# Last expert subtractions ahead of the last norm, token numbers transposed a unit sooner, rank products in f16

## The reference

```python
x = x + wkv(w, u, layernorm(x), ctx)          # k = layernorm(x), v = ctx, recurrence over the 128 times:
#   no = max(o, u+k_t); y = (exp(o-no)*p + exp(u+k_t-no)*v_t) / (exp(o-no)*q + exp(u+k_t-no)); p, q, o updated
h = layernorm(x)                               # 2048 tokens of 512
probs = softmax(h @ gate_w.T)                  # 8 experts
weights, selected = top_k(probs, 2)
moe = sum over the 2 chosen experts e of weight_e * ((silu(h @ G_e.T) * (h @ U_e.T)) @ D_e.T)   # width 256
shared = sigmoid(h @ s.T) * ((silu(h @ G.T) * (h @ U.T)) @ D.T)                                 # width 1024
out = x + moe + shared
```

## Time and profile before

| | us |
|---|---|
| median of 3 timed runs | 570.06 (569.88 to 572.94) |
| the profiled execution | 573.75 |
| its span, first to last instruction | 570.1 |
| TensorE busy | 493.4 (87%) |
| VectorE busy | 423.6 (74%) |
| GpSimd busy | 342.1 (60%) |
| ScalarE busy | 276.4 (48%) |

### The profile page before, as it was taken

The page is one execution under the profiler, slowest core; times in us unless marked ns, Lnnn a source line. Parts: engine busy times, 40 slices in busy tenths (PEclk is TensorE's granted clock), DMA queues, the critical chain, the costliest instruction groups (busy, mean ns, idle before and its releaser), DMA issues.

```text
span 570.1 us, 10205 instructions
## 1 busy us (share of the span) xinstructions
PE 493.4 (87%) x2703; PEld 264.5 (46%) x2703; DVE 423.6 (74%) x954; ACT 276.4 (48%) x534; POOL 342.1 (60%) x421
## 2 busy tenths in 40 slices
PE   1116699899999999999999979899999999999970
PEld 1113345445555555455555544355545555555530
DVE  5778987999989899899898876466656665566650
ACT  4849837475674764756746433433323333333310
POOL 5767946757848578579485364315465665565432
PEclk9999989999999999999999999899999999999995
DMA  7960104115213223052101410305566866576352
GB/s 288 413 259 19 38 18 185 57 27 178 76 56 131 76 103 138 21 185 75 38 20 39 131 60 14 112 20 113 99 108 123 157 114 115 109 127 120 72 75 37
DMA packets 25929, 59.14 MB, mean 104 GB/s; under 512 B 6314, under 2 KB 6314, under 8 KB 24338
## 3 DMA queue, kind: packets, MB, share of 16 engines
q0 software_dynamic: 9824, 20.90, 20.7%
q1 hardware_dynamic: 16050, 37.59, 18.3%
HBM read 37.83 MB, written 20.65 MB: 103 GB/s over the span
## 4 chain that ended last, share of the span: by engine, by line
PE 54%; DVE 14%; issue 11%; POOL 6%; DMA 6%; ACT 5%; SPq 1%; POOLq 0%; DVEq 0%; ACTq 0%
PE GU L882 30%; PE DN L897 14%; DMA out<-wall,idsa 5%; PE XT L827 3%; PE HT L827 3%; ACT wall L700 3%; DVE st L1080 2%; DVE wall L1077 2%; DVE wall L1070 2%; DVE hb L1194 1%; POOL nrm L409 1%; DVE th L1191 1%; DVE xb L1095 1%; SPq L365 1%; POOL xb L572 1%
## 5 line engine op out<-in xcount | busy, mean ns | idle before, releaser
L882 PE MATMUL GU<-wall,xt 128*128 128x512 f16 x768 | 187.9, 385 | 2.1 <-DVE wall L1172 2.0
L897 PE MATMUL DN<-wall,hx 128*128 128x512 f16 (+1 forms) x618 | 151.8, 382 | 6.4 <-DVE hx L1199 4.5
L882 PEld LDWEIGHTS GU<-wall,xt 128*128 128x128 f16 x768 | 75.7, 101 | 70.3 <-issue 4.0
L582 POOL DMA_INDIRECT out<-wall,idsa x39 | 61.8, 1584 | 73.2 <-SPq L369 35.2
L657 ACT ACTIVATE hx<-HT 128x256 f16<-128x256 f32 x103 | 39.0, 379 | 134.3 <-PE HT L827 132.6
L897 PEld LDWEIGHTS DN<-wall,hx 128*128 128x128 f16 x618 | 60.4, 99 | 82.7 <-issue 8.1
L1199 DVE TENSOR_TENSOR hx<-HT,hx 128x256 f16<-128x256 f32 x103 | 43.1, 418 | 65.9 <-ACT hx L657 55.5
L652 ACT ACTIVATE th<-GU,scl 128x256 f32<-128x256 f32 x103 | 48.4, 470 | 77.9 <-PE GU L882 74.9
L882 PE MATMUL GU<-wall,kb 128*128 x240 | 61.4, 379 | 0.2 <-DVE kb L1373 0.2
L572 POOL DMA_INDIRECT xb<-xn_rows,idsi x39 | 40.2, 1030 | 33.1 <-DMA out<-xb 15.6
L882 PE MATMUL GU<-wall,xnb 128*128 x228 | 58.5, 379 | 0.6 <-DVE xnb L1373 0.6
(11 more groups left out here) (162 smaller groups left out, 755.3 us busy)
## 6 DMA issues: line engine op xcount, KB each, us to landing
wall<-wgu SPq DMA_DIRECT2D x12, 1024.0 KB, 9.8
wall<-wd SPq DMA_DIRECT2D x12, 512.0 KB, 10.4
out<-xb SPq DMA_DIRECT2D x20, 256.0 KB, 2.3
xb<-x SPq DMA_DIRECT2D x16, 256.0 KB, 2.8
cb<-ctx_t SPq DMA_DIRECT2D x16, 256.0 KB
xn_rows<-xnb SPq DMA_DIRECT2D x16, 256.0 KB
xb<-xn_rows,idsi POOLq DMA_INDIRECT x39
out<-wall,idsa POOLq DMA_INDIRECT x39
```

Of the source, the lines that this page charges most:

```text
L582: pool.indirect_dma_start(out, bass.IndirectOffsetOnAxis(ap=idsa[:, j:j + 1], axis=0), ye[j % RESULTS], None, compute_op=ALU.add).then_inc ...
L882: ins = nc.tensor.matmul(GU[par][:], lhs(xp, c), gate_up(base, wp, c), start=m == 0, stop=m == 3 * HC - 1)
L897: ins = nc.tensor.matmul(DN[:], hx[par][:, hp * IE + c * P:hp * IE + (c + 1) * P], down(base, wp, c), start=start and m == 0, stop=stop an ...
```

## The change

Four edits. The rank products (`ranks`) take f16 operands, tri16, all16 and an f16 mask, in place of f32 tri, ones and mask; all16 needs one more memset on GpSimd, and tri16 is cut from it. Pieces 1 and 2 of expert 6 (`expert_lo(E - 2, ..)`) stand on GpSimd ahead of the last second norm and of the scatter of tile 12. TensorE's transpose of the token numbers moves from after unit 61 into it, between its hidden transposes and its last six products. On VectorE the copy to yb moves up to stand right behind `experts_of_slots`, and idsi and idsa up to right behind hidden_lo 60; hidden 61 and the accumulate of tile 14 now come behind them.

```diff
-        ident, ones, tri = sb("ident", [P, P]), sb("ones", [P, P]), sb("tri", [P, P])
+        ident, ones = sb("ident", [P, P]), sb("ones", [P, P])
+        all16, tri16 = sb("all16", [P, P], F16), sb("tri16", [P, P], F16)
...
-        ones2, mask, pos2 = sb("ones2", [P, TOPK, E]), sb("mask", [P, E]), sb("pos2", [P, TOPK, E])
+        ones2, mask, pos2 = sb("ones2", [P, TOPK, E]), sb("mask", [P, E], F16), sb("pos2", [P, TOPK, E])
...
             def other_consts():
-                link(pool.affine_select(out=tri[:], in_=ones[:], compare_op=ALU.is_gt, fill=0.0,
+                link(pool.memset(all16[:], 1.0))
+                link(pool.affine_select(out=tri16[:], in_=all16[:], compare_op=ALU.is_gt, fill=0.0,
                                         base=0, pattern=[[1, P]], channel_multiplier=-1))
...
             turns(turn, LAG)
+            expert_lo(E - 2, 1)
+            expert_lo(E - 2, 2)
             norm(B - 1, 1, agg2, norm2, xn_rdy)
             scatter(B - 4)
-            expert_lo(E - 2, 1)
-            expert_lo(E - 2, 2)
...
-                nc.tensor.matmul(LG[:, 16:16 + E], tri[:], mask[:], start=True, stop=True)
-                nc.tensor.matmul(LG[:, 16 + E:16 + 2 * E], ones[:], mask[:], start=True, stop=True).then_inc(ranked, 1)
+                nc.tensor.matmul(LG[:, 16:16 + E], tri16[:], mask[:], start=True, stop=True)
+                nc.tensor.matmul(LG[:, 16 + E:16 + 2 * E], all16[:], mask[:], start=True, stop=True).then_inc(ranked, 1)
...
-            shared_units(B - LAG + 1, last_steps, beyond={3: lambda: gathered_t(0, 0)})
+            shared_units(B - LAG + 1, beyond={1: lists_t, 3: lambda: gathered_t(0, 0)})
```

More of the change, by code:

```diff
@@ L67 @@
 TOP_STEPS, GATE_STEPS, NORM_STEPS, SCALE_STEPS = 3, 1, 3, 10
-CONSTS_FIRST, CONSTS, WKVC = 9, 18, 6
+CONSTS_FIRST, CONSTS, WKVC = 9, 19, 6
 LIST_STEPS, ZEROS, PROBS = 5, 8, 4
@@ L998, in last_of_mix, with lists_t @@
                     sum_squares(1 + E, 2 * SU + 1 + 3 * E, B)
[L1000 to L1004, removed]
+            def lists_t():
+                pe.wait_ge(ids_f, 1)
+                nc.tensor.transpose(KT[:, 0:NSLOT], ids_float, ident[0:NSLOT, 0:NSLOT]).then_inc(ids_t, 1)
             shared_units(B - LAG, last_of_mix, between={0: third_last_ranks},
                          beyond={1: last_router, 2: last_ranks})
-            shared_units(B - LAG + 1, last_steps, beyond={3: lambda: gathered_t(0, 0)})
+            shared_units(B - LAG + 1, beyond={1: lists_t, 3: lambda: gathered_t(0, 0)})
             def expert_of(j):
@@ L1401, in _ @@
             experts_of_slots()
-            hidden_lo(n, 0)
-            hidden(n + 1, 1, SHARED)
-            accumulate(B - 2)
             dve.wait_ge(ids_ld, 16)
@@ L1407, in _ @@
                                   ).then_inc(ids_f, 1)
+            hidden_lo(n, 0)
             dve.wait_ge(ids_t, 1)
@@ L1411, in _ @@
             TT(idsa[:], KT[:, 0:NSLOT], pad_of[:], ALU.add).then_inc(ids_rdy, 1)
+            hidden(n + 1, 1, SHARED)
+            accumulate(B - 2)
             hidden_lo(n + 1, 1)
```

## The result

| | before | after |
|---|---|---|
| median of the timed runs, us | 571.50 (569.88 to 575.62) | 565.32 (564.55 to 566.33) |
| ratio, with 95% interval | | 0.9883 [0.9842, 0.9923] |
| span of the profiled execution, us | 570.1 | 564.3 |
| mix: from TensorE's transposes of y of tile 4 to those of tile 15, us | 209.82 | 207.41 |
| from there to the first slot's transposes, us | 42.41 | 39.18 |

The change makes the kernel faster by 6.2 us in the medians and by 5.8 us in the spans. Forecast were 563.2 us and 6.9 us less; the time lies in the forecast range of 560.8 to 567.0. The median before is now of four runs, one of them (575.62 us) new beside the changed kernel. Of the 2.1 us between 563.2 and 565.32, 1.4 are this raised median and 0.7 are saving that was missed.

The account below looks back on a forecast made before the run. TensorE was taken to bound the mix, VectorE close behind. 3.8 + 0.55 + 0.4 + 2.97 = 7.7 us off the 570.1 span gave 562.4; with about half the clock's 1.7, the median forecast was 563.2 us, range 560.8 to 567.0.

Parts of the forecast that it names:

- rank products in the mix: TensorE, turns 3 to 15: 13 pairs in f16 save 0.29 us each, 3.8 us; upper bound 4.0.
- norm and subtractions, at the router: Tail: last norm 2.7 us late, but router's last product starts at 336.4 instead of 336.97, saving 0.55 us.
- rank pairs of tiles 14 and 15: Behind the last norm: tile 14's pair saves 0.29 us, tile 15's waits for the mask; 0.4 us in all.
- token numbers: Tail: earlier transpose brings hidden transposes 2.97 us sooner, 1.7 of it the fallen clock, 1.27 order.
- slots: The 39 slots behind the tail follow TensorE's progress, so what is won before them is passed on.
- the room of VectorE: In the mix, hb is ready 0.53 us before its transpose, more than one turn's 0.29 us saving.
- Rival (2): VectorE takes over in the mix, shorter rank products only lengthen TensorE's wait; only the tail counts, 567.0 us; chance 0.15.
- Rival (3): Slower: GpSimd's subtractions hold VectorE's small steps 2.13 us; one hit in each of 12 turns gives 582 us; chance 0.05.
- Rival (4): The late norm keeps TensorE from the router as long as held VectorE did, saving 0 there; 563.8 us; chance 0.07.
- Rival (1): The clock falls behind the new 2.8 us idle in most runs, seldom in the old; 565.8 us; chance 0.18.

Follow-up runs that it names:

- piece_later: The kernel after, with piece 1 of each expert subtracted on GpSimd in the next, odd turn; ratio 0.9948 to the kernel before.
- all_four: The kernel after with norm_between's and free_first's edits, and piece_later's except that the last piece 1 stays in its turn; 562.52 us, ratio 0.9832 to the kernel before.
- norm_only: The kernel before with only GpSimd's last two expert subtractions moved ahead of the last norm and scatter; 570.03 us, ratio 0.9975.
- norm_between: The kernel after, with the last norm between GpSimd's two last expert subtractions instead of behind both; 562.32 us, ratio 0.9853 to the kernel before.
- between_and_free: The kernel after with the edits of both norm_between and free_first; 563.24 us, ratio 0.9844 to the kernel before.
- between_before: The kernel before with the last norm between the two last expert subtractions, the scatter behind both; 569.49 us, ratio 0.9964.
- drag_odd: The kernel after, with two more f32 products ahead of the rank pair in the odd turns of the mix; ratio 0.9937 to the kernel before.
- drag_even: The kernel after, with two more f32 products ahead of the rank pair in the even turns of the mix; ratio 0.9951 to the kernel before.
- free_first: The kernel after, with tile 14's accumulate ahead of hidden 61 on VectorE; 565.73 us, ratio 0.9893 to the kernel before.
- ranks_only: The kernel before with the f16 rank products alone; 567.85 us, ratio 0.9942.
- tokens_only: The kernel before with only the token numbers' transpose and VectorE's steps around it moved; 569.79 us, ratio 0.9969.

## Why the prediction came out as it did

The sum forecast a span of 562.4 us; it is 564.3. By its own terms, from the starts of TensorE's operations (the second term ends with the product behind the router's, the third with the one behind the last rank pair):

| term | forecast, us | measured, us |
|---|---|---|
| rank products in the mix | 3.8 | 2.69 |
| norm and subtractions, at the router | 0.55 | 0.42 |
| rank pairs of tiles 14 and 15 | 0.4 | 0.14 |
| token numbers | 2.97 | 2.66 |
| slots | 0 | -0.12 |
| sum | 7.7 | 5.8 |

**Rank products.** The price was right: 0.05 us in f16. As an estimate by the Trainium skill, page "TensorE: Matmul & The Clock Gate", section "LDWEIGHTS (loading the stationary operand)", the pair would have taken 0.11 to 0.21 us; the rows at 318.19 don't agree. Each of the two weight loads takes 0.10 us in the trace, near the 107 ns that the page's rule gives, but the loads overlap, and the products follow each other at 0.025 us. The step that failed is "the next operations of VectorE and ScalarE start from TensorE's results, so they move with it". It holds for a pair of turns as far as 37.80 us (18.9 a turn, forecast 18.8); then GpSimd's even turn is late. I had read the room of VectorE in one turn (0.53 us) and of GpSimd in none. Of 4.0 us (13 x 0.31) 1.3 are not passed on. Relieving GpSimd gave 0.8 of them back by tile 14 (piece_later); neither piece_later nor all_four kept it to the end of the mix. Rival (2) had the right effect in part and named the wrong engine: the new waits are for GpSimd, and VectorE as the bound was not shown. Rival (3) did not come: the longest hold of a small VectorE step in the mix behind tile 3 is 1.32 us (L1137 at 226.97), and holds of 1.10 us were there before.

**Norm.** TensorE idles 3.19 us ahead of XT (forecast 2.8), the router's product waits for nothing, and 0.42 us stay. Rival (4) was that nothing stays; norm_only shows it to be right further on: at the token numbers that edit alone has gained nothing. VectorE's L1154 is 0.17 us, and L1137 and L1157 are held for 0.61 and 1.84 us where 2.5 were forecast for one. The Trainium skill, page "SBUF — State Buffer", section "Who interferes with whom", lets whichever issues first hold the ports for its whole instruction. In the kernel after the rows agree: L1137 waits for the end of the first piece, L1147 gets in beside the second, and L1157 waits for the end of that one. The 4.22 us of L1153 in the kernel before went over two pieces.

**The pair of tile 14.** The forecast let it start as before. It waits 0.30 us, for a ScalarE step I had not looked at:

```profile
334.08 0.38 ACT L659 ACTIVATE hx<-HT 128x256 f16<-128x256 f32 x1 [2.21 <-PE HT L829]
335.52 0.27 ACT L640 ACTIVATE lga<-LG,scl 128x9 f32<-128x9 f32 x1 [1.06 <-PE LG L856]
```

lga starts 1.64 us behind the router's product (333.88 to 335.52), where it started 0.49 us behind it in the kernel before (336.97 to 337.46). The trace puts the idle down to that product, though its twelve parts had gone by at 334.18. It is so in all six kernels that reach the router without a wait and at full clock (after, norm_only, norm_between, between_and_free, all_four, between_before: 1.56 to 1.68 us). The copy of HT right ahead of lga on ScalarE does not explain it: drag_odd, drag_even, piece_later and free_first have it too, and lga starts 0.48 or 0.49 us behind the product. In all six lga starts 0.01 to 0.14 us ahead of the end of VectorE's accumulate, in those four before it begins. But in before, ranks_only and tokens_only the two run side by side. So the cause stayed open.

**Token numbers.** KT waits 0.24 us (forecast 0.27), the down products 1.00 (0.82). 1.7 of the 2.66 us are a clock that had fallen in the kernel before and not here; ranks_only and between_before, where it had not fallen, confirm the 1.7 (7.11 and 7.10 us from KT to the first slot for 8.80). Order gave 0.96 of the forecast 1.27. The down products start 3.76 us behind the product after KT (352.15 to 355.91), forecast 3.42: that is the 0.3. (The forecast's 2.12 us, 358.41 less 356.27, is 2.14.) That a fallen clock stood in the one profile and not in the other was luck, and it makes up 1.7 of the 5.8 us between the spans; the forecast had said so and put only half of it into the median.

**The clock.** Rival (1) had 0.18. The profile of after decides against it (1.00 between 330 and 340 us), but the runs of the same tail do not: with 2.9 to 3.2 us idle ahead of XT it fell in four profiled kernels of six (drag_odd, drag_even, piece_later, free_first; not in after and norm_only), at 1.6 to 2.7 us each up to the router's product; 0.24 of it came back by the token numbers' transpose (17.84 us from the router's product for 18.08), as lga was not late there. The chance should have been near one half. The four timed executions of after have spans of 562.8, 562.8, 564.3 and 564.6, which would fit a clock fall more or less; only the profiled one, 564.3, can be read, and it has a fall near 72 us, worth 1.6, as the kernel before has.

## What to carry to other kernels

A saving on the busiest engine is worth its full price only until the next engine's longest turn is late; look for that engine over a whole period of the loop, and at all engines, not at the room of one. When a short urgent step and two long ones share an engine, try the place between the long ones as well as both ends: here that was worth 1.8 us more, where standing behind both had given 0.4 at the router and, by itself, lost it again. And an idle of 2 to 3 us on TensorE can cost more than itself, so a wait that is shortened is worth more than one that is moved. Before an experiment with single traces is read, look at how far two kernels with the same code in that stretch differ: here up to 1.1 us.

## What the runs showed of the hardware

- Whether the clock falls behind an idle is not settled by the code in this kernel. Behind 2.9 to 3.2 us idle it fell in six of nine profiled kernels and stayed at 1.00 in three; behind 2.37 us in two of four, behind 2.57 us in the only one, and near 72 us, behind 2.1 to 2.2 us, in six of thirteen (0.66 from 72.4 to 77.4 us, in the others 1.00). Where one kernel's trace has it fallen and the other's not, 1.0 to 2.7 us of their difference say nothing of the change. Behind 0.8 to 1.1 us ahead of XT it never fell, in four kernels.
- GpSimd's operations on one value per partition take 0.19 us, and 1.03 to 1.16 us when VectorE's scans run beside them. With its start 1.2 us sooner, the same chain took 0.33 us longer.
- VectorE gets in between two subtractions of GpSimd that stand back to back in one case (L1147 at 326.33, after) and not in another (L1153, 4.22 us, before).
- Products of a 128x128 f16 weight with 8 columns follow each other at 0.025 us; the same pair in f32 takes 0.34 to 0.37 us, not twice but some seven times as much.
